# Gelu low halves moved from VectorE to GpSimd in a fused MLP with residual, float32 in split precision

## The reference

```python
h = gelu(x @ fc1_w.T + fc1_b)                      # 256 -> 1024, exact Gelu
shared = h @ fc2_w.T + fc2_b                       # 1024 -> 192
expert = h @ experts_w[index].T + experts_b[index] # 1024 -> 64, weights by row
out = x + concatenate([shared, expert], -1)
```

## Time and profile before

| | |
|---|---|
| median of three runs | 382.38 us |
| the profiled execution: span from its first to its last instruction | 380.7 us |
| the profiled execution's own time | the page gives its span and no other time; the median of the runs is 1.7 us above that span |
| mean granted TensorE clock | 0.985 of full speed |
| busiest engine | TensorE |

### The profile page before, as it was taken

The page is one execution under the profiler, slowest core; times in us unless marked ns, Lnnn a source line. Parts: engine busy times, 40 slices in busy tenths (PEclk is TensorE's granted clock), DMA queues, the critical chain, the costliest instruction groups (busy, mean ns, idle before and its releaser), DMA issues.

```text
span 380.7 us, 5936 instructions
## 1 busy us (share of the span) xinstructions
PE 368.8 (97%) x1841; PEld 309.5 (81%) x1841; DVE 217.0 (57%) x331; ACT 196.5 (52%) x266; POOL 57.1 (15%) x27
## 2 busy tenths in 40 slices
PE   4799999999999999999999999999999999999996
PEld 4587877888888888888888888888888888888885
DVE  1289477656556556655655665565565566556442
ACT  2297356555554655555455454546546554653520
POOL 1023121230120303012030300203030030302000
PEclk9599999999999999999999999999999999999999
DMA  6932987444240523324052441415234151300011
GB/s 137 250 77 85 305 149 196 144 104 126 60 141 26 140 88 96 131 58 143 27 133 94 96 131 46 127 54 134 94 89 138 43 130 55 89 28 29 28 37 47
DMA packets 64516, 39.08 MB, mean 103 GB/s; under 512 B 37338, under 2 KB 63722, under 8 KB 64506
## 3 DMA queue, kind: packets, MB, share of 16 engines
q1 hardware_dynamic: 63584, 35.41, 34.1%
q0 software_dynamic: 880, 3.54, 3.6%
q10 hardware_dynamic: 42, 0.00, 0.0%
HBM read 27.40 MB, written 8.39 MB: 94 GB/s over the span
## 4 chain that ended last, share of the span: by engine, by line
PE 86%; DVE 5%; DMA 5%; ACT 2%; SPq 2%; issue 1%
PE fc_ps L593 40%; PE acc_ps L629 29%; PE acc_ps L631 15%; DMA resid<-in_L_cond_fc_w 2%; DVE ht L466 2%; DMA pieces<-in_L_cond_experts_w 2%; SPq L174 1%; ACT ht L343 1%; PE fc_ps L601 1%; DVE tr_ps L411 1%; PE fc_ps L565 1%; ACT gelu L338 0%; SPq L218 0%; DVE xt L404 0%; ACT w2t L305 0%
## 5 line engine op out<-in xcount | busy, mean ns | idle before, releaser
L593 PE MATMUL fc_ps<-xt,w1t 128*128 128x512 f32 x762 | 194.2, 394 | 0.0
L629 PE MATMUL acc_ps<-w2t,ht 128*128 128x512 f32 x512 | 185.1, 398 | 1.3 <-DVE resid L485 0.8
L593 PEld LDWEIGHTS fc_ps<-xt,w1t 128*128 128x128 f32 x762 | 135.6, 188 | 28.8
L466 DVE TENSOR_TENSOR ht<-gelu,ht 128x1024 fp32r<-128x1024 f32 x64 | 83.2, 1301 | 130.2 <-ACT ht L343 130.2
L338 ACT ACTIVATE gelu<-fc_ps,b 128x512 f32<-128x512 f32 x128 | 88.2, 690 | 131.5 <-PE fc_ps L593 127.8
L631 PE MATMUL acc_ps<-w2t,ht 128*128 128x256 f32 x512 | 143.5, 280 | 0.0
L629 PEld LDWEIGHTS acc_ps<-w2t,ht 128*128 128x128 f32 x512 | 96.2, 188 | 26.0 <-DVE w2t L404 1.8
L631 PEld LDWEIGHTS acc_ps<-w2t,ht 128*128 128x128 f32 x512 | 96.6, 189 | 3.9
L260 POOL TENSOR_TENSOR resid<-x_in,bias 128x1024 f32<-128x1024 f32 x16 | 51.0, 3190 | 282.0 <-DMA out<-resid 251.5
L343 ACT ACTIVATE ht<-gelu 128x1024 fp32r<-128x1024 f32 x64 | 67.9, 1062 | 2.0
L481 DVE TENSOR_TENSOR resid<-acc_ps,resid 128x256 f32<-128x256 f32 x64 | 26.8, 419 | 7.5 <-PE acc_ps L631 7.5
(11 more groups left out here) (27 smaller groups left out, 35.3 us busy)
## 6 DMA issues: line engine op xcount, KB each, us to landing
x_in<-in_x SPq DMA_DIRECT2D x16, 512.0 KB, 4.6
pieces<-in_L_cond_experts_w SPq DMA_DIRECT2D x128, 64.0 KB, 2.0
out<-resid SPq DMA_DIRECT2D x30, 256.0 KB, 2.2
pieces<-in_x SPq DMA_DIRECT2D x56, 128.0 KB, 2.8
w2t<-w2t POOLq DMA_DIRECT2D x4, 768.0 KB, 8.6
resid<-in_L_cond_fc_w SPq DMA_DIRECT2D x8, 128.0 KB, 7.0
bias<-in_L_cond_experts_b SPq DMA_DIRECT2D x32, 32.0 KB, 3.5
pieces<-in_L_cond_fc_w SPq DMA_DIRECT2D x4, 192.0 KB, 4.9
```

The lines of the kernel that those rows point to most:

```text
L466: nc.vector.tensor_tensor(ht[:, par, LO, 2 * r:2 * r + 2, :].rearrange("p k t -> p (k t)"), gelu[:, r % 2, :], ht[:, par, HI, 2 * r:2 * r ...
L593: last = nc.tensor.matmul(fc1_ps[:, j % FC1_BANKS, :], w1t[:, d, w, js], xt[:, par, d, v, :], start=(at == 0), stop=(at == len(terms) - 1))
L629: nc.tensor.matmul(acc_ps[:, bank, :], ht[:, par, HI, k, ts], w2t[:, par, t // T, k, :], start=(k == 0), stop=False)
```

## The change

`pair_lo` goes from VectorE's program to GpSimd's. It is the same subtraction on the same tiles, in the same number (64). On GpSimd it has one wait more, for the matmuls of block i-2, which read the low halves that it overwrites. GpSimd gets a step with four turns: the low halves of pair r of block i+1, and, behind that of pair 2, `residual` of block i+2. VectorE's other work stays in its order.

```diff
@@ gpsimd
+            def pair_lo(i, par, r):
+
+                pool.wait_ge(h_hi, HALF * i + r + 1)
+                if not (isinstance(i, int) and i < 2):
+
+                    pool.wait_ge(acc_filled, 1 + TILES * (i - 1))
+                nc.gpsimd.tensor_tensor(
+                    ht[:, par, LO, 2 * r:2 * r + 2, :].rearrange("p k t -> p (k t)"),
+                    gelu[:, r % 2, :],
+                    ht[:, par, HI, 2 * r:2 * r + 2, :].rearrange("p k t -> p (k t)").bitcast(FP32),
+                    ALU.subtract).then_inc(h_lo, 1)
+
+            def step(i, par, use, more=True):
+
+                for r in range(HALF):
+                    pair_lo(i + 1, 1 - par, r)
+                    if r == 2 and more:
+                        residual(i + 2, par, use)
...
             residual(0, 0, 0)
+            for r in range(HALF):
+                pair_lo(0, 0, r)
 
 
             pool.wait_ge(acc_drained, ACC_FIRST)
...
             residual(1, 1, 0)
+            step(0, 0, 1)
             with pool.Fori(0, PAIRS) as m:
-                residual(2 * m + 2, 0, m + 1)
-                residual(2 * m + 3, 1, m + 1)
-            residual(BLOCKS - 2, 0, BLOCKS // 2 - 1)
-            residual(BLOCKS - 1, 1, BLOCKS // 2 - 1)
+                step(2 * m + 1, 1, m + 1)
+                step(2 * m + 2, 0, m + 2)
+            step(BLOCKS - 3, 1, BLOCKS // 2 - 1)
+            step(BLOCKS - 2, 0, 0, more=False)
@@ vector
-            def pair_lo(i, par, r):
-
-                dve.wait_ge(h_hi, HALF * i + r + 1)
-                nc.vector.tensor_tensor(
...
                 for r in range(HALF):
                     h = r % 2
-                    pair_lo(i + 1, 1 - par, r)
...
-            pair_lo(0, 0, 0)
             shared_lo(2)
             x_lo(1, TR_X1, 0, 0)
-            pair_lo(0, 0, 1)
...
             shared_square(3)
-            pair_lo(0, 0, 2)
...
             shared_square(4)
-            pair_lo(0, 0, 3)
```

## The result

The kernel with the change takes 448.52 us in the median of four runs (446.54 to 450.78), the kernel before 382.27 in the median of four. The ratio is 1.174, 95% interval 1.171 to 1.177: 17% slower, 66 us. The profiled execution of the kernel after took 450.78 us, the longest of the four; its span is 448.9.

What follows compares the result with a forecast made beforehand. TensorE, busy 97% of 380.7 us, was taken as the bound. 380.7 + 39 (steps) + 11.5 (start) + 3 (clock) - 1 (waits for VectorE) = 433 us span, so 435 predicted for the median, range 424 to 462.

Steps and rivals of the forecast that it cites:

- The bound and the order: In each step: TensorE bounds; GpSimd's load, 12.0 of 22.3 us, does not, but its order makes pair 3 late.
- The price of an operation: On GpSimd: each subtraction and each residual takes 2.40 us, bounds 1.23 and 3.47.
- The chain from the seam: Between steps: additions, store, residual, pair 3 need 8.4 us against 5.4 of cover; TensorE 3.0 late, 13 times, 39 us.
- The start: At the kernel's start: TensorE gets pair 3 11.5 us late, bounds 8.5 and 13, plus 3 us for the clock.
- the place of residual 1: At the start: pair 0 of block 1 waits behind residual 1 and ends at 55.05; VectorE did it at 38.03.
- The step that failed: In steady steps: the clock stays full after each stop of 3.0 us, so nothing was added for it.
- Rival 1: In every step: the clock falls, losing 1.5 to 3.0 us each, 20 to 39 in 13 steps: 455 to 474; chance 0.20.
- Rival 2: On GpSimd: operations stay at 3.47 us, 2.1 us more a step, some 3 at the start: 465; chance 0.07.
- Rival 3: In the steps and start: not slower, the chain ends within TensorE's 5.4 us: 381; chance 0.03.
- Rival 4: In each step: late by only 1 to 2 us, with a lighter start: 400 to 424; chance 0.08.
- the tests that I named: In the profile after: about 50 us idle for GpSimd's subtraction, steps of 25.3, TensorE's share 86%, residual 3.3 after last product.
- the test on the clock: In the profile after: clock at half after the gap near 60 to 70 us, full after the others.

Runs made afterwards that it cites:

- experiments 1 and 5: Kernel with the change, but residual i+2 behind pair 3: 389.91 us; kernel with the change, but pair 3 back on VectorE except block 0: 387.39 us.
- experiment 6: Kernel with the change, but only pair 3 of each block except block 0 on GpSimd, behind the residual, all other pairs on VectorE: 467.05 us.
- experiment 2: Kernel with the change, but residual 1 behind pair 1 of block 1 instead of ahead of pair 0: 449.36 us, ratio 1.177.

## Why the prediction came out as it did

- **The bound and the order: right.** TensorE does wait for pair 3, once a step, at tile 0's second half; experiments 1 and 5 show that pair 3's place behind the residual is the steady cost, and nothing else of the move, and experiment 6 that it alone is enough.
- **The price of an operation: right.** I took 2.40 us; the 64 subtractions lie between 2.33 and 2.41 us, the 16 residuals too. The residuals that were 3.3 to 3.5 were those that met VectorE's L466, and with that gone so is the length. The Trainium skill (SBUF — State Buffer, "Who interferes with whom") has the rule that a VectorE instruction with two inputs in SBUF and a GpSimd one that reads SBUF exclude each other, and that one with at most one input there, outside VectorE's two-port modes, doesn't contend. By it the rest of VectorE's steady work is harmless, and the trace agrees: 80 operations, none above 2.41. Experiment 6 brought the meeting back, with 3.34.
- **The chain from the seam: right to 0.2 us.** I had first addition 0.31 behind the start of the last matmul (0.32: 117.48 to 117.80), store and landing 2.40 (2.46: 118.67 to 121.13), two operations 4.80 (4.70, to 125.8), TensorE going on at 125.98. TensorE late by 3.0 became 2.87 (25.18 - 22.31), 13 times 37 us for my 39.
- **The start: right in sum, in part by luck.** 11.5 and 3 for the clock made 14.5; measured 14.2. The terms were each off: TensorE used pair 3 at 71.91, 12.7 us behind the 59.20 of the earlier trace rows and not 11.5, and 1.5 more came behind that, for my 3 of the clock. I had one gap of about 10 us; there were two, 3.7 and 6.2, with the clock at half after each (0.84 in the mean of step 1). And the place of residual 1, which I had put at the head of the path, adds little: experiment 2 takes it away, block 0's store still lands at 64.86 (65.22 before), and TensorE goes on 2.3 us sooner. It is residual 2 and pair 3 behind that store that cost.
- **The step that failed** is the clock, which I had put at nothing in the steady steps. Rival 1 had it fall "in every step". The runs show a mixture, 10 of 13 steps (2 to 14) at 1.6 us each, 16 us, and this is nearly the whole distance between the forecast for the span, 433, and the 448.9 measured. I had given the rival 0.20 and 1.5 to 3.0 us a fall. My argument against it, that dense products stand on both sides, was wrong at 2.65 us; the table shows that the clock stays up at 1.6. Its row for it, the fall within 1.7 us of a stop, pointed the right way, though there the work before was lighter. The Trainium skill (TensorE: Matmul & The Clock Gate, "HAM oscillation — how this bites in real kernels") tells of a clock thrown back at every tile by waits of about 3 to 5 us, and I was wrong to read from it that a stop of 3.0 must do the same; here it is so at 3.65 and 5.1 us, in most steps at 2.65, which is shorter than the waits it tells of, and not at 1.6.
- **Rival 2** (3.47 us an operation) didn't come, for the reason above. **Rival 3** (not slower) needed a chain under 5.4 us; it took 8.2. **Rival 4** (late by only 1 to 2 us) didn't come either.

Of the tests that I named most held: idle time of the group with GpSimd as its releaser 42.2 for "about 50" (the 3.7 us missing from the long gap are a wait for ScalarE), TensorE's share 87% for 86%, residual 3.4 us behind the end of the last product (117.76 to 121.13), pair 3 directly behind it. The steps of 25.3 are there, but are the minority, and the test on the clock, full after every gap but the one near 60 to 70 us, failed.

## What to carry to other kernels

Work that moves to an idle engine takes on all the waits of that engine's program. Write down for each instruction ahead of the moved one what it waits for and when that comes; here one line further down was worth 59 us, and the engine's load, 12 of 22 us, said nothing about it. And price a stop of TensorE with the clock in mind: a delay of 2.9 us became 4.5 in most steps (26.8 - 22.3), and filling the stop with thrown-away matmuls won 12.8 us, where taking it away won 59.

## What the runs showed of the hardware that I had not expected

The clock fell after the stop was over: TensorE resumed at 125.98 at full speed, was put to half at about 126.5, and ran so for 3.4 us, though it was busy all that time. After stops of the same length, 2.65 to 2.7 us, it fell in 8 of 11 steps (3 to 13) and not in the other 3, in one execution. Their order isn't random: from step 3 on the fall comes 0.5 and 1.0 us after the stop's end, then there is none, then at 0.3, 0.8 and 1.3, none, 0.6 and 1.2, none, 0.4 (from the granted clock in the trace); experiment 2 has the same pattern. So when the stop comes seems to matter beside how long it is; no run here tests that. And of two instructions that block each other the later one waits out the earlier, and the third in line waits too (experiment 6: 2.12 us for 1.23 on VectorE, then 3.34 for 2.40 on GpSimd), so that a clash of two engines can reach a further instruction of the first.
